# Cross-attention and experts on one core: three PSUM banks for the softmax scores and two for everything else, with a new TensorE order

## What is computed

```python
q = layernorm(x) @ Wq.T + bq            # 16 batches, 224 x 512
k = context @ Wk.T + bk                 # 750 x 512
v = context @ Wv.T + bv
attn = softmax(einsum('bihd,bjhd->bhij', q, k) / sqrt(32))
x = x + einsum('bhij,bjhd->bihd', attn, v).reshape(...) @ Wo.T + bo
x = x + experts(layernorm(x))           # top 2 of 8, not touched by the change
```

## Time and profile before

| | |
|---|---|
| median of the runs | 1845.82 us (1843.85 to 1850.29, 3 runs) |
| profiled execution | 1845.75 us, its span 1843.9 us |
| TensorE matmul busy | 1581.9 us (86%) |
| TensorE weight load busy | 1290.4 us |
| VectorE busy | 1106.7 us |
| ScalarE busy | 940.9 us |
| POOL busy | 1078.7 us |

### The profile page before, as it was taken

How to read it: one execution, slowest core, us unless ns; L and a number is a source line. 1 busy time by engine, 2 the same in 40 slices (tenths; PEclk the granted TensorE clock), 3 DMA queues, 4 the chain that set the end, 5 groups by cost and what they waited for, 6 DMA issues and landing times. The chain is left out here.

```text
span 1843.9 us, 32950 instructions
## 1 busy us (share of the span) xinstructions
PE 1581.9 (86%) x11655; PEld 1290.4 (70%) x11655; DVE 1106.7 (60%) x1853; ACT 940.9 (51%) x2053; POOL 1078.7 (59%) x715
## 2 busy tenths in 40 slices
PE   5899999999999999999999999998534327999992
PEld 4777777777777777777777777776334325998892
DVE  5566667666666666666666666665165666555551
ACT  4556656565565656656565565654111111555551
POOL 3466766676665766756676665765422231777771
PEclk9899999999999999999999999998655555999996
DMA  7466666657576586666657576576153251888887
GB/s 199 67 120 84 132 113 113 132 87 143 96 126 113 92 153 85 130 111 111 134 86 142 99 124 120 88 117 95 44 184 116 95 183 43 147 150 145 150 151 193
DMA packets 108509, 221.76 MB, mean 120 GB/s; under 512 B 12576, under 2 KB 37440, under 8 KB 108112
## 3 DMA queue, kind: packets, MB, share of 16 engines
q1 hardware_dynamic: 90368, 174.28, 50.2%
q0 software_dynamic: 17984, 45.39, 12.7%
HBM read 81.03 MB, written 49.94 MB: 71 GB/s over the span
## 5 line engine op out<-in xcount | busy, mean ns | idle before, releaser
L674 DVE TENSOR_REDUCE mx<-X 112x1 f32<-112x752 f32 x512 | 481.3, 940 | 364.0 <-PE X L864 363.7
L313 POOL TENSOR_TENSOR psum_p<-psum_p,pr 125x896 f32<-125x896 f32 x256 | 541.6, 2116 | 217.6 <-ACT pr L491 189.7
L491 ACT ACTIVATE pr<-S 125x448 f32<-125x448 f32 x768 | 389.7, 540 | 189.7 <-PE S L887 182.0
L887 PEld LDWEIGHTS S<-qst,kst 128*125 128x125 f32 x1536 | 237.5, 190 | 94.5 <-ACT pr L491 47.6
L887 PE MATMUL S<-qst,kst 128*125 128x224 f32 x1536 | 283.3, 289 | 22.3 <-ACT pr L491 17.9
L864 PE MATMUL X<-kh_s,q_own 128*112 128x376 f32 x1024 | 277.2, 352 | 26.8 <-DVE mx L674 26.7
L310 POOL TENSOR_TENSOR psum_p<-pr 125x896 f32<-125x896 f32 x64 | 137.4, 2146 | 141.7 <-ACT pr L491 141.7
L864 PEld LDWEIGHTS X<-kh_s,q_own 128*112 128x112 f32 x1024 | 152.0, 177 | 81.7 <-DVE mx L674 47.6
L903 PE MATMUL O<-pr,v 125*32 125x224 f32 x3072 | 188.8, 364 | 1.8 <-ACT pr L491 1.8
L1284 POOL DMA_INDIRECT acc<-xTf,table_i x70 | 111.3, 1591 | 63.1 <-ACT xTf L1341 57.4
L202 PE MATMUL M<-ctx_l,wk_h 128*128 128x376 f32 (+1 forms) x384 | 129.8, 338 | 0.0
(11 more groups left out here) (198 smaller groups left out, 3225.5 us busy)
## 6 DMA issues: line engine op xcount, KB each, us to landing
kst<-kh_s SPq DMA_DIRECT2D x128, 375.0 KB, 6.9
kst<-kl_s SPq DMA_DIRECT2D x64, 375.0 KB, 10.7
ctx_r<-ctxT SPq DMA_DIRECT2D x48, 375.0 KB, 11.0
qst<-qh_s SPq DMA_DIRECT2D x128, 112.0 KB, 2.9
stage<-w POOLq DMA_DIRECT2D x16, 512.0 KB, 5.4
xn_d<-rows SPq DMA_DIRECT2D x7, 1040.0 KB, 5.0
x_ln<-x SPq DMA_DIRECT2D x16, 448.0 KB, 11.4
x_res<-x SPq DMA_DIRECT2D x16, 448.0 KB, 13.0
```

What stands on the lines that cost most here:

```text
L313: pool.tensor_tensor(out=total, in0=total, in1=tiles[half], op=ALU.add).then_inc(sum_step, 1)
L491: act.activation(pr[0:KP, (3 * g + p) % 2, j, :, :], S[0:KP, n % SB, 0:2 * NQ].rearrange("p (i n) -> p i n", i=2), ACT.Exp).then_inc(exp_d ...
L674: dve.tensor_reduce(mx[0:QP, u:u + 1], X[0:QP, :, 0:HALF[0][1]], AX.XY, ALU.max).then_inc(max_done, 1)
L887: last = pe.matmul(S[0:KP, n % SB, NQ * h:NQ * (h + 1)], kst[:, i, j, o:o + KP], qst[:, i, j, :], start=True, stop=True)
```

## The change

S gets three banks and M two, so `score` may run three exponentials ahead, and every unit of M waits for the unit two before it instead of three. `misc_units` is changed to the new order of units: V4 ahead of den in the first kind of group, K1 ahead of V0 in the third. TensorE's four lists are written in a new order; the steps in them are the same, and VectorE, ScalarE, POOL and SyncE keep their lists. The diff, whole:

```diff
--- before.py
+++ after.py
@@ -63,7 +63,7 @@
 
 
 GROUPS = B * NG
-SB, MB = 2, 3
+SB, MB = 3, 2
 OS = 5
 XU = 8
 LAST = 2
@@ -77,13 +77,13 @@
     for g in range(-2, GROUPS + LAST):
         t, b = g % NG, g // NG
         if t == 0:
-            order += [("Q", g + 2), ("K0", g + 2), ("K1", g + 2), ("den", g - 1), ("V4", b), ("V5", b),
+            order += [("Q", g + 2), ("K0", g + 2), ("K1", g + 2), ("V4", b), ("den", g - 1), ("V5", b),
                       ("mT", g + 1)]
         elif t == 1:
             order += [("Q", g + 2), ("K0", g + 2), ("K1", g + 2), ("xT0", b + 1), ("xT1", b + 1), ("den", g - 1),
                       ("O0", b - 1), ("O1", b - 1), ("mT", g + 1)]
         elif t == 2:
-            order += [("Q", g + 2), ("K0", g + 2), ("V0", b + 1), ("K1", g + 2), ("den", g - 1), ("V1", b + 1),
+            order += [("Q", g + 2), ("K0", g + 2), ("K1", g + 2), ("V0", b + 1), ("den", g - 1), ("V1", b + 1),
                       ("mT", g + 1)]
         elif t == 3:
             order += [("Q", g + 2), ("K0", g + 2), ("K1", g + 2), ("den", g - 1), ("V2", b + 1), ("V3", b + 1),
@@ -946,100 +946,100 @@
                     score_for_max(g + 1, 1)
                     values(g - 1, 2)
                     score(g, 0)
+                    score(g, 1)
                     score_for_max(g + 1, 2)
                     project_k(g + 2, 1)
-                    score(g, 1)
                     score(g, 2)
+                    score(g, 3)
                     score_for_max(g + 1, 3)
-                    denominators(g - 1)
-                    score(g, 3)
-                    score(g, 4)
                     project_v(b, 4, 0)
                     project_v(b, 4, 1)
+                    denominators(g - 1)
+                    score(g, 4)
+                    score(g, 5)
                     project_v(b, 5, 0)
-                    score(g, 5)
                     score_for_max(g + 1, 4)
                     project_v(b, 5, 1)
                     score_for_max(g + 1, 5)
                     score(g, 6)
                     score(g, 7)
+                    score(g, 8)
+                    score_for_max(g + 1, 6)
                     values(g, 0)
-                    score_for_max(g + 1, 6)
-                    score(g, 8)
-                    score(g, 9)
-                    values(g, 1)
-                    score_for_max(g + 1, 7)
-                    score(g, 10)
-                    score(g, 11)
-                    transpose_max(g + 1)
-
-                def second(g, b):
-                    score_for_max(g + 1, 0)
-                    project_q(g + 2)
-                    values(g - 1, 2)
-                    score_for_max(g + 1, 1)
-                    score(g, 0)
-                    project_k(g + 2, 0)
-                    score_for_max(g + 1, 2)
-                    score(g, 1)
-                    score(g, 2)
-                    project_k(g + 2, 1)
-                    score_for_max(g + 1, 3)
-                    score(g, 3)
-                    transpose_x(b + 1, 0)
-                    transpose_x(b + 1, 1)
-                    values(g, 0)
-                    denominators(g - 1)
-                    score(g, 4)
-                    project_o(b - 1, 0, 0)
-                    score_for_max(g + 1, 4)
-                    score(g, 5)
-                    score(g, 6)
-                    score(g, 7)
-                    score_for_max(g + 1, 5)
-                    project_o(b - 1, 0, 1)
-                    project_o(b - 1, 1, 0)
-                    score_for_max(g + 1, 6)
-                    score(g, 8)
-                    score(g, 9)
-                    values(g, 1)
-                    score(g, 10)
-                    score_for_max(g + 1, 7)
-                    score(g, 11)
-                    project_o(b - 1, 1, 1)
-                    transpose_max(g + 1)
-
-                def third(g, b):
-                    score_for_max(g + 1, 0)
-                    project_q(g + 2)
-                    values(g - 1, 2)
-                    score_for_max(g + 1, 1)
-                    score(g, 0)
-                    project_k(g + 2, 0)
-                    score_for_max(g + 1, 2)
-                    score(g, 1)
-                    project_v(b + 1, 0, 0)
-                    project_k(g + 2, 1)
-                    score(g, 2)
-                    score_for_max(g + 1, 3)
-                    score(g, 3)
-                    project_v(b + 1, 0, 1)
-                    denominators(g - 1)
-                    score(g, 4)
-                    score_for_max(g + 1, 4)
-                    project_v(b + 1, 1, 0)
-                    score(g, 5)
-                    project_v(b + 1, 1, 1)
-                    score_for_max(g + 1, 5)
-                    values(g, 0)
-                    score(g, 6)
-                    score_for_max(g + 1, 6)
-                    score(g, 7)
-                    score(g, 8)
                     score(g, 9)
                     score_for_max(g + 1, 7)
                     values(g, 1)
                     score(g, 10)
+                    transpose_max(g + 1)
+                    score(g, 11)
+
+                def second(g, b):
+                    score_for_max(g + 1, 0)
+                    project_q(g + 2)
+                    project_k(g + 2, 0)
+                    score_for_max(g + 1, 1)
+                    values(g - 1, 2)
+                    score(g, 0)
+                    score(g, 1)
+                    score_for_max(g + 1, 2)
+                    score(g, 2)
+                    project_k(g + 2, 1)
+                    score_for_max(g + 1, 3)
+                    transpose_x(b + 1, 0)
+                    score(g, 3)
+                    score_for_max(g + 1, 4)
+                    transpose_x(b + 1, 1)
+                    score(g, 4)
+                    score(g, 5)
+                    denominators(g - 1)
+                    values(g, 0)
+                    project_o(b - 1, 0, 0)
+                    score(g, 6)
+                    score_for_max(g + 1, 5)
+                    score(g, 7)
+                    project_o(b - 1, 0, 1)
+                    score(g, 8)
+                    score_for_max(g + 1, 6)
+                    score(g, 9)
+                    project_o(b - 1, 1, 0)
+                    score(g, 10)
+                    score(g, 11)
+                    score_for_max(g + 1, 7)
+                    project_o(b - 1, 1, 1)
+                    transpose_max(g + 1)
+                    values(g, 1)
+
+                def third(g, b):
+                    score_for_max(g + 1, 0)
+                    values(g - 1, 2)
+                    project_q(g + 2)
+                    score(g, 0)
+                    score_for_max(g + 1, 1)
+                    project_k(g + 2, 0)
+                    score_for_max(g + 1, 2)
+                    project_k(g + 2, 1)
+                    score(g, 1)
+                    score(g, 2)
+                    score(g, 3)
+                    score_for_max(g + 1, 3)
+                    project_v(b + 1, 0, 0)
+                    project_v(b + 1, 0, 1)
+                    denominators(g - 1)
+                    score_for_max(g + 1, 4)
+                    score(g, 4)
+                    score(g, 5)
+                    project_v(b + 1, 1, 0)
+                    score(g, 6)
+                    project_v(b + 1, 1, 1)
+                    score_for_max(g + 1, 5)
+                    values(g, 0)
+                    score(g, 7)
+                    score_for_max(g + 1, 6)
+                    score(g, 8)
+                    score(g, 9)
+                    score(g, 10)
+                    score_for_max(g + 1, 7)
+                    values(g, 1)
                     score(g, 11)
                     transpose_max(g + 1)
 
```

## The result

The changed kernel is slower: 1856.85 us median (1853.37 to 1861.52, 7 runs) against 1844.92 (1841.9 to 1850.29, 7 runs), a ratio of 1.0067 with a 95% interval of 1.005 to 1.0084. I had forecast 1835, faster; the measured time lies just inside the wide range of 1813 to 1858, on the wrong side of before. Its profiled execution took 1853.37 us (span 1851.6), the fastest of its seven runs.

What follows compares the result with a forecast made beforehand. TensorE's own work (busy 96%) plus short waits bounds attention. Groups of 20.2 + 21.15 + 18.45 + 18.35 = 78.15 against 78.77 us, 0.62 x 15.75 = 10 less: 1835 us; own range 1828 to 1841, eight in ten 1813 to 1858.

Steps and rivals of the forecast that it cites:

- sum: The four groups of a batch added: 78.15 us against 78.77 before, 0.62 x 15.75 = 10 us less.
- clock: No term of its own: TensorE was read as at full clock, and waits were priced by length alone.
- Third score bank: Scores may run three exponentials ahead; removes score waits only where X 5 does not wait for the same normalise.
- banks for the rest: Two banks: each claim waits for the unit two before; nothing at best (x transpose 0.2), 0.94 us each if a maximum intervenes.
- Fourth group: X 5's wait for normalise falls from about 1.4 to 0.1 us; the group takes 18.35, 1.5 less.
- First group, the block: POOL's addition holds normalise until 14.0 us, X 5 at 15.15, new wait 1.6; group 20.2, 1.3 more.
- Third group: Den at 9.9 us, den to X 5 3.7 without a wait; group 18.45, 0.4 less.
- Second group: Score waits of 1.4 us go, but X 4, x transpose and X 5 waits cost 1.4: 21.15, nothing gained.
- the slip: Rival, chance 0.2: normalise beats POOL's addition in the first group, group 19.15, 1.05 us less each batch, 1818 us.
- The banks bind: Rival, chance 0.19: bank releases through VectorE come 0.3 us or more later than counted; 1853 to 1881, taken as 1862 us.
- The wait only moves: Rival, chance 0.19: score waits become X waits in all four groups, fourth group's gain halves; batch 0.1 longer, 1848 us.

Runs made afterwards that it cites:

- e9: Changed kernel plus five unused 512-column matmuls on TensorE ahead of X 5 of the first group: 1845.77 us, ratio 1.001.
- e1: Changed kernel; in the first group POOL's addition 0 also waits for VectorE's normalise: 1834.77 us, ratio 0.9942.
- e2: Changed kernel; in the first group POOL's addition 0 waits for the low part of the output: 1823.89 us, ratio 0.9883.
- e6: Kernel before, old order, with three score banks and two for the rest: 1890.51 us, ratio 1.0236.
- e4: Kernel before; in the fourth group POOL's addition 0 waits for normalise: 1830.28 us, ratio 0.9926.

## Why the prediction was wrong, point by point

The forecast of 1835 failed in two terms: the **sum** of the four groups, 78.15 us where 79.3 were measured, and the **clock**, which it put at nothing. On the medians they are about equal: the fill of e9, which ends the spells, gives 1845.77, so 10.8 of the 21.9 us belong to the sum and 11.1 to the clock. The mechanisms that it named held, by the steps of the text:

- *Third score bank*, *banks for the rest*: right for this order. Score waits nearly went, and the x transpose waited its 0.2 us.
- *Fourth group*: 18.35 forecast, 18.45 measured.
- *First group, the block*: forecast X 5 at 15.15, measured 15.14, and e1 and e2 show that this addition on POOL makes it. That the addition starts 0.37 us ahead of normalise was a close call, as the prediction says. The Trainium skill (SBUF — State Buffer, Who interferes with whom) states that a VectorE instruction with two SBUF inputs contends with a GpSimd instruction that reads SBUF. The traces agree: normalise stands for 1.98 us until POOL's addition ends, the low part for 1.68 in e1, and e2 has them at 0.39 and 0.44 us. What followed X 5 was sized at 5.05 and took 5.4. X 6 came 1.73 behind X 5, not 1.55, which the prediction had named as a sign of being wrong: after the wait it is 0.64 instead of 0.54 from X 5 to its maximum (782.13 to 782.77), and X 6 starts 0.15 after that maximum's end instead of 0.06. The rest is 0.07 more from X 6 to values and 0.07 at the end. 20.2 forecast, 20.5 measured.
- *Third group*: 18.45 forecast, 18.98 measured. From den to X 5 it was 3.70 as forecast. Den came at 10.2 instead of 9.9, although "the same work precedes den": the rows of before already give 9.98 (652.88 - 642.90), X 0 takes 0.52 ahead of values where it took 0.41 ahead of the queries, and X 2 starts 0.1 late, its weight load waiting for ScalarE's `q_own`, a wait that the forecast did not have (the row below the list). 5.1 us followed X 5 instead of 4.85: X 7 takes 0.54 after its own wait, not 0.43, and the transpose's 0.12 had been left out.
- *Second group*: 21.15 forecast, 21.36 measured. Start to start, over the 0.21 of the score ahead of it, X 4 came 0.75 late and X 5 0.7, for 0.55 and 0.65.

```profile
653.74 0.27 PEld L864 LDWEIGHTS X<-kh_s,q_own 128*112 128x112 f32 x2 [0.21 <-ACT q_own L448]
```

Each was too low by 0.1 to 0.5; together 79.3 against 78.15. What an operation costs depends on what stands next to it (X 0 above), and I had given each one price for the whole order; why the neighbours matter was not tested. The term was a difference of two large sums, 0.62 us in 79, and the prices were good to about 1.5%: the range of 1828 to 1841 which I gave it was too narrow for that.

**Left out: the clock.** I gave the wait of 1.6 us in the first group its length as its price. Five of fourteen such waits in the profiled execution, the fastest of seven, also cost 1.5 us of half speed: 7.4 us. The other six runs have a lower mean granted clock (0.917 to 0.919 against 0.922), and e9 puts the whole at 11 us of the median. That is nearly all of the measured loss of 12 against the kernel before: with the spells gone the change is worth nothing either way (1.001).

**Where the profiled 7.6 us come from.** The batches 1 to 14 took 79.86 us on average against 78.90, 13.4 in all where I had forecast 8.7 less; 7.4 of it are the spells. The one batch that I had read as the base took 78.77, 0.13 less than that average. The first batch took 2.0 less (81.19 before, 79.17 after), the last three groups 4.6 less (58.82 before, 54.20 after), which a fixed saving for each of 15.75 batches could not show; other ends make up the rest. In e9 the 63 groups took 1244.8 us, before 1244.9.

The rivals: *the slip* did not happen: the addition started 0.37 us ahead of normalise, forecast 0.3. e1 made it happen and gave 19.75, forecast 19.15: its addition starts only at 12.7, when normalise is done, so the low part was held longer. *The banks bind*, my slower case, named the right side by the wrong cause: in this order the claims cost what I counted, and only the old order (e6) is bound by them. *The wait only moves* was nearest in kind: in the first and second group it is just what happened.

## What to carry to other kernels

- When a hand-written order is rebuilt, look for pairs of VectorE and POOL instructions that read SBUF at the same time, as well as counting banks: in both kernels the longest idle time of TensorE in a usual batch (1.37 us in the fourth group before, 1.47 in the first after) came from an addition on POOL that nobody was in a hurry for, running over a short step on the critical chain. Holding the unhurried one back was worth 0.7% in the old order (e4) and, ahead of the low part, 1.8% in the new one (1856.85 to 1823.89, e2), about a third of that through the clock (11 of 33 us by e9).
- Price a new idle stretch of TensorE with its clock as well as its length; where it can't be removed, spare matmuls in it are a way to see which of the two it is.
- A forecast made as a small difference of two long sums needs the error of the sums as its range, and the first and last groups counted by themselves.

## What the runs showed of the hardware

Idle stretches as short as 1.47 and 0.48 us, 1.2 us of work apart, came ahead of a spell at the lower clock in five batches, while the nine others, most with the same idle times to 0.02 us, had none; with 2.3 us idle thirteen of fourteen had one. A single stretch of 1.37 us (the fourth group of the kernel before) or of 1.29 (the first in e1) had none behind it in any batch: the clock of both kernels is 1.00 from 120 to 1280 us. Whether the 0.1 us or the second stop makes the difference was not separated. A spell cost 1.5 us where the wait was 1.6, and 0.9 (22.29 - 21.35) to 3.0 (24.32 - 21.35) at the longer one. Whether a given wait is hit changes from batch to batch, and the mean clocks of the seven runs suggest that their number changes from run to run.
